# A two-layer attention and expert kernel: another order of its steps, with batch 1's expert layer between batch 0's second and third attention, and reciprocal buffers for the second attention

## The reference, cut to what matters

```python
x = x + L0_xattn(layernorm(x), ctx)   # 16 heads of 8 channels, 77 keys
x = x + L0_ffn(layernorm(x))          # router, top 2 of 8 experts, hidden 256
x = x + L1_xattn(ctx, layernorm(x))   # 16 heads, 77 keys, + residual, layernorm
x = x + L1_ffn(layernorm(x))          # 16 heads, 512 keys, rope; then shared and
                                      # routed experts on an rmsnorm; rmsnorm
```

## Time and profile before

| | us |
|---|---|
| median of 3 runs | 346.26 |
| the runs | 345.16, 346.26, 735.23 |
| the profiled execution | 346.35 |
| its span in the trace | 344.5 |
| mean granted TensorE clock | 0.976 of full speed |

### The profile page before, as it was taken

One profiled execution on the slowest core, in us unless ns is written; L12 is line 12 of the kernel. 1 busy time (PEld: TensorE's weight loads), 2 busy tenths in 40 slices (PEclk: granted clock), 3 DMA queues, 4 the chain that ended last, 5 costly groups with the idle time before them and its releaser, 6 DMA issues.

```text
span 344.5 us, 5997 instructions
## 1 busy us (share of the span) xinstructions
PE 311.3 (90%) x2249; PEld 159.1 (46%) x2249; DVE 268.3 (78%) x687; ACT 213.6 (62%) x260; POOL 70.8 (21%) x130
## 2 busy tenths in 40 slices
PE   3789999999999997986988999999999999999980
PEld 1555545877685562563522225342232343644530
DVE  2788867723788868789999999999988835489895
ACT  3549887674867874626853976988798996002100
POOL 4154420100200374213172151011011200011001
PEclk9999999999999997889999999999999999999996
DMA  6930000000000000000000000000000000000001
GB/s 194 430 142 3 3 0 3 0 2 0 3 0 2 0 2 1 2 0 3 0 2 1 2 0 0 2 2 0 2 0 2 2 2 0 0 0 2 1 0 61
DMA packets 1900, 7.48 MB, mean 22 GB/s; under 512 B 208, under 2 KB 336, under 8 KB 1488
## 3 DMA queue, kind: packets, MB, share of 16 engines
q1 hardware_dynamic: 1872, 7.11, 5.3%
HBM read 6.58 MB, written 0.52 MB: 21 GB/s over the span
## 4 chain that ended last, share of the span: by engine, by line
PE 56%; DVE 21%; issue 11%; ACT 9%; POOL 1%; DMA 1%; POOLq 0%; SPq 0%; ACTq 0%; DVEq 0%
PE ring_ps L596 32%; PE out_ps L596 11%; DVE mx L1185 8%; ACT pT L969 5%; PE misc_ps L596 4%; DVE ACC L1361 3%; PE misc_ps L809 2%; PE ring_ps L716 1%; PE misc_ps L754 1%; DVE ACC L1034 1%; PE misc_ps L630 1%; DVE Z L1034 1%; DVE bn L1044 1%; ACT qT L961 1%; PE ring_ps L809 1%
## 5 line engine op out<-in xcount | busy, mean ns | idle before, releaser
L969 ACT ACTIVATE pT<-ring_ps 128x1024 f32<-128x1024 f32 (+1 forms) x96 | 94.2, 1027 | 24.2 <-PE ring_ps L596 23.3
L1185 DVE TENSOR_REDUCE mx<-ring_ps 128x2 f32<-128x1024 f32 (+1 forms) x96 | 98.8, 1074 | 7.7 <-PE ring_ps L596 7.2
L596 PE MATMUL ring_ps<-XT,f 128*128 128x512 f32 x96 | 44.3, 601 | 0.0
L525 POOL TENSOR_TENSOR rstd<-var,consts 128x4 f32<-128x4 f32 x14 | 14.8, 1056 | 136.6 <-DVE var L1052 75.7
L596 PE MATMUL out_ps<-pT,V 128*32 128x512 f32 x256 | 34.9, 605 | 0.0
L564 POOL TENSOR_SCALAR pT<-pT 77x1024 f32<-77x1024 f32 x8 | 22.7, 2848 | 47.8 <-ACT pT L969 47.8
L596 PE MATMUL ring_ps<-f,hid 128*128 128x512 f32 (+1 forms) x96 | 31.9, 487 | 0.0
L1361 DVE SCALAR_TENSOR_TENSOR X<-ring_ps,gw,X 128x128 f32<-128x128 f32 x64 | 18.0, 344 | 16.8 <-PE ring_ps L596 16.5
L596 PEld LDWEIGHTS ring_ps<-f0y,hid 128*128 128x128 f32 x256 | 29.6, 192 | 2.4 <-issue 1.9
L596 PE MATMUL ring_ps<-f0y,hid 128*128 128x128 f32 x256 | 30.4, 276 | 0.0
L596 PE MATMUL ring_ps<-kT,qT 48*128 48x512 bf16 x128 | 24.1, 384 | 2.3 <-DVE mx L1185 1.3
(11 more groups left out here) (184 smaller groups left out, 460.2 us busy)
## 6 DMA issues: line engine op xcount, KB each, us to landing
f<-in_f SPq DMA_DIRECT2D x1, 1669.0 KB, 15.0
f<-in_f SPq DMA_DIRECT2D x1, 1028.0 KB, 8.8
f0y<-in_f0y SPq DMA_DIRECT2D x1, 1024.0 KB, 10.8
X<-in_x SPq DMA_DIRECT2D x2, 256.0 KB, 4.7
wb<-in_wb SPq DMA_DIRECT2D x1, 512.0 KB, 11.6
rows<-in_rows SPq DMA_DIRECT2D x1, 512.0 KB, 11.3
trig<-in_trig SPq DMA_DIRECT2D x1, 512.0 KB, 11.7
out<-ACC SPq DMA_DIRECT2D x2, 256.0 KB, 2.0
```

The source lines that it names most:

```text
L525: return pool.tensor_tensor(out, a, c, op)
L596: return nc.tensor.matmul(out, lhsT, rhs, start=start, stop=stop)
L969: nc.scalar.activation(probs_buf(layer, i, kt)[0:parts_, 2 * half:2 * half + 2, :], ring_ps[ring.buf(step)][0:parts_, :, :], ACT.Exp, scal ...
L1185: V_.tensor_reduce(dst, src, AX.X, ALU.max).then_inc(ring.read_sem(step), 1)
```

## The change

The four tables `ORDER`, `BORROWING`, `KEPT_BUSY` and `FILLED` are replaced, and the second attention's reciprocals get four buffers of their own, `rinv1`, instead of the four that all attentions share. No step is added or removed: the order has the same 493 steps. The products of the identity go from 103 to 84 (59 and 44 to 40 and 44). Of the tables a line or two is shown.

```diff
@@ KEPT_BUSY, FILLED: first lines
-KEPT_BUSY = {("QP", 0, 0): 3, ("QT", 0, 0, 0): 6, ("SMAX", 0, 0, 0, 0): 4, ("MTR", 0, 0): 1, ("ST", 0, 0, 0, 0): 2,
+KEPT_BUSY = {("QP", 0, 0): 2, ("SMAX", 0, 0, 0, 0): 4, ("MTR", 0, 0): 1, ("ST", 0, 1, 0, 0): 2, ("XT", "z0", 0): 1,
...
@@ ORDER: two of its lines
-    QT 1 0 1, FH 1 4, SMAX 1 0 0 0, SMAX 1 0 0 1, SMAX 1 1 0 0, FH 1 5, MCH 1 0, SMAX 1 1 0 1, SMAX 1 2 0 0,
+    FH 1 3, FH 1 4, FY 1 2, NORM n4 0, FY 1 3, FY 1 4, XT n4 0, QP 2 0, KV 0, SPLITK 0, FH 1 5, FH 1 6, FH 1 7,
...
@@ BORROWING: its second line
-    XT z0 1, OP 0 1, XT n1 1, RT 1, QP 1 1, XT n4 0, MTR 1 6, MTR 2 7, OTR 2 6, OTR 2 7, XT z2 1, OP 2 1
+    OTR 0 7, QP 1 0, WKV, XT z0 1, MTR 1 0, RT 1, QP 2 0, OTR 2 0, MTR 2 3, MTR 2 7, OTR 2 5, OP 2 1
...
@@ buffers, and OTR of the second attention
         rinv = [sb(f"rinv{i}", [P, T, HG]) for i in range(GR)]
+        rinv1 = [sb(f"rinv1_{i}", [P, T, HG]) for i in range(GR)]
...
-                    inv = rinv[i % GR][:, :, :].rearrange("p t j -> p (t j)")
+                    inv = rinv1[i % GR][:, :, :].rearrange("p t j -> p (t j)")
```

More of the change, by code:

```diff
@@ L155 @@
+    RO 0 1 0, XT fl 1, RO 0 1 1, STAT r2 0, GH 1 0, NORM r2 0, GT 1, GH 1 1, OUT 0, SO 1, GTE 1, RO 1 0 0, RO 1 0 1,
+    RO 1 1 0, RO 1 1 1, STAT r2 1, NORM r2 1, OUT 1
 """
 BORROWING = """
-    XT n0 0, XT n0 1, QP 0 1, MTR 0 1, MTR 0 3, OTR 0 3, MTR 0 6, MTR 0 7, OTR 0 4, XT n1 0, OTR 0 6, OTR 0 7,
-    XT z0 1, OP 0 1, XT n1 1, RT 1, QP 1 1, XT n4 0, MTR 1 6, MTR 2 7, OTR 2 6, OTR 2 7, XT z2 1, OP 2 1
+    CKV 0, QP 0 1, OTR 0 0, MTR 0 4, OTR 0 3, OTR 0 2, MTR 0 5, CKV 1, XT n1 0, RT 0, OTR 0 4, OTR 0 6, XT n2 0,
```

110 lines of the change are left out of this document (54 added, 56 removed), and 7 rows, old and new, of tables (FILLED, KEPT_BUSY).

## The result

| | us |
|---|---|
| changed kernel, median of 9 runs | 350.48 (346.66 to 353.69) |
| kernel before beside it, median of 9 | 345.92 (344.09 to 347.9, and one run of 735.23) |
| ratio to the kernel before | 1.0091, 95% interval 1.0052 to 1.013 |
| the profiled execution, its span | 347.54, 345.8 |

The account below looks back on a forecast made before the run. Different engines bound the kernel in turn; the change could win only by shrinking 50.3 us of VectorE gaps. Span 344.5 - 2.2 - 0.3 = 342.0 us, + 1.85 outside = 343.8 us; range 335 to 350.5.

Parts of the forecast that it names:

- Stage A: Start to batch 0's last expert product: forecast to end at 79.9 us, 6.0 us earlier than before.
- Stage B: Batch 0's second attention: first maximum at 95.5 us, then 25.4 us to the output norm's statistics, ending at 120.9 us.
- hidden: Batch 0's second attention: GpSimd's four guards, 2.85 us each, run in succession, end at about 18 us and add no time.
- warning sign: Stated sign that the forecast is wrong: the granted clock falls ahead of the expert products after 110 us.
- turning point: Batch 0's second attention, first maximum to norm statistics: a loss once it takes over 28 us instead of 25.4.
- Stage C: Batch 0's norm statistics to first maximum of its third attention: 30.9 us against 32.2 before, ending at 151.8 us.
- Stage D: Batch 0's third attention with batch 1's second inside: 76.3 us, batch 1's first maximum at 228.1 us, 2.2 earlier.
- the change of batch: In Stage D: 1.5 us added because 5 maxima instead of 7 cover GpSimd's and ScalarE's part of the chain.
- The rest: From batch 1's first maximum of the third attention on: both orders about the same, 0.3 us gained in the tail.
- Fits better: Rival, 26%: Stage B and Stage C pack VectorE's 58.5 us of work tighter than 70.6 us, 6 to 8 less; 336.5 us.
- Stage B doesn't keep TensorE going: Rival, 18%: batch 0's second attention alone leaves TensorE idle, the clock falls for about 7 us; 353.5 us.
- The third: Rival, 14%: in Stage D VectorE waits 3 to 4 us for batch 1's chain; 347 us, no change.

## Why the prediction was wrong, by its own steps

**Stage A: the times came true, in part by luck.** Output projection until 44.1 us (44.2 forecast), first hidden layer at 50.84 (51.1), last expert product at 80.0 (79.9). But the profile that the forecast started from has 1.8 us of half rate in its start and the changed kernel's has 0.9, from the stretch near 16 us. Between the two runs without GpSimd's guards, both at full rate from 9.3 us on, the projection ends 3.0 us earlier (46.2 to 43.2; 3.9 forecast) and the last expert product 4.9 (84.0 to 79.1; 6.0 forecast). The stretch near 16 us isn't due to the six identity products that the transposes lost: the run without batch 1's guards has the same products and no such stretch.

**Stage B: the step that failed, and the larger part of the miss.** The way to the first maximum held (95.7 for 95.5). From there the prediction summed VectorE's rows at their prices of before, 22.4 us and 3 of waits, 25.4, and called GpSimd's guards "hidden". The walk was even too long, for without those guards the stage takes 23.6. What failed is the word hidden: GpSimd's four guards, put back to back by the new order, cost 2.5 us by overlap (26.1), 0.3 or less by being waited for (26.4 with batch 0's guards whole and no fall; stage C, which no guard touches, varies by as much between runs), and the fall of the clock 1.7 more (28.1). The prediction also walked this stage at full-clock prices and expected no half clock between 80 and 230 us, while the profile it started from had two falls there. Its own warning sign, a fall ahead of the expert products after 110 us, is the one at 115. That part is not bound to the guards: it is missing in a run with the same four guards. The turning point that the prediction gave, "over 28 us instead of 25.4", was reached; but by other causes in part than the rival named, for the clock fell for 3.4 us, not for 7.

**Stage C: right**, 30.5 for 30.9.

**Stage D: the same step again.** Forecast 76.3, measured 79.0; without GpSimd's guards 75.8, with the overlap and no fall 77.4, with the fall at 166 us under batch 1's query transposes (32 of them in 2.56 us, VectorE waiting 2.05) 79.0. The sum of its other terms, with 14.4 us of work moved in and 1.5 for the change of batch, is borne out by the 75.8; the terms were not tested one by one.

**The rest: 1.4 us better than forecast** (112.5 for 113.9). ScalarE has 48.95 us of work from the first maximum of batch 1 to 291.6 where it had 51.64: it seems to be further ahead with the exponentials at the boundary, which no run tests. The prediction had taken both orders for equal there. The place of `OUT 0` was not tested.

**The sum.** 342.0 forecast, + 2.7 (B) - 0.4 (C) + 2.7 (D) - 1.4 (rest), with 0.2 from the start, gives the 345.8 of the span. Of the 5.4 us of the two stages, some 4.1 plus 0.3 are overlap and waiting and 3.3 half clock, less 2.3 by which the walk was too long. Overlap and waiting, 4.4 us, are about what the walk had too long in B, D, C and the rest (4.1), so that in this one execution the miss of 3.8 us is as large as its half clock (0.9 in the start and 3.3). The overlap is the part that every trace of the changed order with these guards shows. The profiled execution is one of the changed kernel's quicker ones; its median lies 2.9 us higher, in runs whose mean clock is 0.964 to 0.975 instead of 0.977. Those runs have no trace, so what they lose, and where, stays open; a forecast made on one profile can't see that spread.

**The rivals.** "Fits better" was right on VectorE and undone by GpSimd: without the guards the change is 1.5% faster (95% interval 0.4 to 2.5, 4 runs). Its 70.6 us for stages B and C is a slip: by the prediction's own terms it is 71.9. "Stage B doesn't keep TensorE going" had the right place and the right sign, with too large a price. The third, a wait of 3 to 4 us in stage D for batch 1's chain, did not come: without GpSimd's guards D took 75.8 us, 0.5 less than the walk. The prediction's row for GpSimd's guard was read as a duration and an idle time to spare; what it does to the neighbour was not asked, although the trace of before had two hints in rows that were not read: router and split rows of 0.2 us that took 0.91 and 1.00 us, the one beside GpSimd's bias addition, the other at the start of a guard. In the timeline of VectorE, kernel before:

```profile
93.91 0.91 DVE L1034 TENSOR_TENSOR gv<-gex,gv 128x4 f32<-128x4 f32 x1
...
114.59 1.00 DVE L1034 TENSOR_TENSOR qcat<-mrs,qcat 128x16 bf16<-128x16 f32 x1
```

And of GpSimd:

```profile
93.50 1.30 POOL L525 TENSOR_TENSOR X<-X,rows 128x512 f32<-128x512 f32 x1 [3.49 <-ACT XN L896]
114.47 2.77 POOL L564 TENSOR_SCALAR pT<-pT 77x1024 f32<-77x1024 f32 x1 [19.67 <-ACT pT L969]
```

## What to carry to other kernels

A reordering that closes the gaps of one engine makes engines overlap that did not before: ask not only what an instruction costs and when it runs, but which instructions it will now run beside, and look in the old trace for rows of one form whose times differ. Time on GpSimd "for nothing" is not for nothing beside VectorE; leave the instruction out once, put one in that nobody waits for, and the difference of the two separates overlap from latency. Where a kernel is held at full clock by filler products, a new order moves the falls as well, and a fall can also come in one run and stay out in the next with the same instructions and the same waits. So compare stage lengths with and without a fall, and look where each trace's clock record begins, before believing a gain or a loss of 1%.
